# Doubling the self-attention keys over the partitions in the projection, from weights stored twice, in place of four SBUF transfers per head pair

## The chip, the cores and the metric

The kernel runs on one core of one Trainium2 chip. The metric is device time of one execution in microseconds (us). The core's engines are TensorE (PE in the profile, with its weight loads as PEld), VectorE (DVE), ScalarE (ACT), GpSimd (POOL) and SyncE (SP), which here only issues transfers to the 16 DMA engines.

## What is computed

Two decoder layers over x of shape 4 x 1024 x 256, one batch row after the other. The change touches one of the six blocks, the causal self-attention of the second layer, and the set-up of its weights:

```python
def _L1_attn_ref(x, w_q, w_k, w_v, w_o):          # w_*: 16 heads x 64 x 256
    q = jnp.einsum('bsd,hqd->bhsq', x, w_q)
    k = jnp.einsum('bsd,hqd->bhsq', x, w_k)
    v = jnp.einsum('bsd,hvd->bhsv', x, w_v)
    scores = jnp.einsum('bhsq,bhtq->bhst', q, k)
    ...
    weights = jax.nn.softmax(masked / jnp.sqrt(jnp.float32(dq)), axis=-1)
    out = jnp.einsum('bhst,bhtv->bhsv', weights, v)
    return jnp.einsum('bsf,df->bsd', cat, w_o)
```

The other blocks (an attention on random features, a cross-attention and a mixture of experts in layer 0, a cross-attention and a quantized gated network in layer 1) are the same before and after.

## The kernel before

**Precision.** Products of float32 numbers are built from two rounded parts, an upper and a lower one. `mm3` (L231) issues three matmuls per product: upper by upper, upper by lower, lower by upper. So a projection of 512 tokens with 256 inputs takes 2 x 3 = 6 matmuls of 128 x 512 (L233 to L235).

**The stage.** Heads are worked in eight pairs; a pair's projection fills 128 partitions, 64 for each head. The scores of a head must multiply (upper q + lower q) by k. The contraction of a matmul runs over the partitions, and a head has only 64 values, so a head's upper q lies on one half of the partitions and its lower q on the other (L1348, L1441). The keys must then be there twice, once on each half. The upper keys come by transfers: ScalarE copies the projection of the pair from PSUM into `l_x` (L1344; `l_x` is a part of `xn`, and the trace calls it xn), and SP issues four transfers per head pair (`l_dup`, L1508), which write each head's 64 rows to both halves of `l_k1`. The lower keys `l_k2` stand on their own half alone; the other half is zero, set by GpSimd at the stage's start.

**Steps and slots.** A head pair is one step of 16 blocks of 128 queries (two heads, eight blocks in the order 7, 0, 6, 1, 5, 2, 4, 3). I call the place k = 0 to 15 of a block in its pair a slot. A block passes: scores on PE (L1268 to L1270), row maximum on DVE (L1382), exponential on ACT (L1333), upper half-precision part on POOL (L1491), lower part on DVE (L1388), a DMA transpose (`l_flip`, L1500), and the product with the values on PE (L1286). Each engine runs its own list in order, written out by hand. In slot k PE issues the scores of the block six ahead, then a side task if the slot has one, then the product with the values of block k. DVE takes the maximum of the block six ahead, the side task's part, then the lower part of the block four ahead. SP issues the transpose of the block four ahead, then whatever else stands in that slot.

**Side tasks** (`l_tasks`, L1133) make what the next pair needs: K and Q (two each, one per 512 tokens), T (the output turned, two), and four of V (odd pairs) or O (even pairs from 2 on). All go through one PSUM bank, number 5. For each, PE waits until the task before has left the bank (L1305), issues its matmuls (`l_make`), ACT copies the upper part (`l_make_upper`), and DVE takes the lower part and frees the bank (`l_make_lower`). In pair 0 only K and Q have side tasks. The last pair has tasks of the next block in place of K and Q.

**Start.** Before the first scores the tasks of `FIRST_BANK` run: K, Q and V of the first pair, each in a bank of its own.

**Set-up.** The weights are split into parts once, and SP stores them to DRAM (`setup_split_sp`, L1769). ACT waits for these stores before `x_a_kv` in the first batch row (L1984). The stage loads a pair's weights from there, 512 KB at a time (`l_load_w`, L1511).

## Time and profile before

| | |
|---|---|
| Time, median of 3 runs | 3016.09 us (3014.46 to 3021.33) |
| Profiled execution, its own time | 3017.71 us |
| Its span, first to last instruction | 3016.0 us |
| Busy share of the span | PE 76%, DVE 72%, PEld 61%, ACT 35%, POOL 19% |
| Granted TensorE clock, mean | 0.864 of full speed |
| Head-pair steps 0 to 6 of the four stages | 279.3, 278.5, 282.7 and 278.1 us |

Times in the rows are microseconds from the span's start, unless marked ns. A step is counted from the first row maximum of one head pair to that of the next. The view of busy time by stretch has these columns: the stretch, its length, then busy time (and count of instructions) of PE, PEld, DVE, ACT and POOL, then the granted clock, the busy share of the DMA engines and the GB/s that they moved. In the groups by line, the number after the bar is the busy time, then the mean of one instruction in ns, then the engine's idle time just before these instructions and what ended it. On SP a row's time is that of issuing the transfer, not of the transfer.

### The profile page before, as it was taken

To read this page: it belongs to the slowest core of one execution; us is meant where nothing else is said; L and a number is where in the kernel's file an instruction comes from. 1 tells how busy PE (TensorE), PEld (TensorE's weight loads), DVE (VectorE), ACT (ScalarE), POOL (GpSimd) and SP (SyncE) were. 2 spreads that over 40 slices of the span, in tenths; PEclk is the share of its full clock that TensorE was granted. 3 is DMA by queue.
4 is the path that set the end of the run, shared out by engine and by line. 5 is a ranking of instruction groups with operands and counts; after the bars stand their busy time and mean duration, and the time that the engine had idled before them with its cause. 6 is when DMAs were issued, how large, how long until landed. Compare 5 with 4: busy or idle time off the path is not lost.

```text
span 3016.0 us, 50608 instructions
## 1 busy us (share of the span) xinstructions
PE 2279.5 (76%) x17454; PEld 1839.1 (61%) x17470; DVE 2179.1 (72%) x4246; ACT 1059.6 (35%) x2004; POOL 587.7 (19%) x666
## 2 busy tenths in 40 slices
PE   3668778868667778886777777887777777888875
PEld 3557666657455766665655666666556566666664
DVE  6765788867766578886776667888686756888766
ACT  2312444422522244442242234444134223444324
POOL 2011222212001122221201122222110102222120
PEclk8778899988778889998887789999887888999888
DMA  6001799830001089982000128997000014889600
GB/s 234 1 16 39 139 163 170 160 76 1 1 15 55 15 161 169 166 149 47 1 10 6 55 58 153 167 169 139 22 1 15 1 55 97 165 165 154 111 1 14
DMA packets 658403, 251.34 MB, mean 83 GB/s; under 512 B 613082, under 2 KB 633946, under 8 KB 657370
## 3 DMA queue, kind: packets, MB, share of 16 engines
q1 hardware_dynamic: 653978, 243.79, 41.2%
q10 hardware_dynamic: 4160, 4.19, 0.4%
q8 instruction: 144, 2.36, 0.3%
q14 instruction: 121, 0.99, 0.1%
...
## 4 chain that ended last, share of the span: by engine, by line
issue 32%; PE 26%; DVE 19%; DMA 11%; ACT 5%; POOL 4%; DVEq 1%; SPq 1%; ACTq 0%; POOLq 0%
PE ps L233 6%; DMA l_ptb<-l_phb 5%; PE ps L235 5%; PE ps L234 5%; DMA l_pts<-l_phs 4%; DVE nmax L1382 3%; POOL d_pn L990 2%; PE ps L1286 2%; DVE l_k L1437 1%; DVE l_phb L1388 1%; DVE l_q L1441 1%; PE ps L1268 1%; ACT l_q L1348 1%; DVE l_phs L1388 1%; DVE xn L284 1%
## 5 line engine op out<-in xcount | busy, mean ns | idle before, releaser
L1382 DVE TENSOR_REDUCE nmax<-ps 128x1 f32<-128x1024 f32 (+7 forms) x512 | 383.9, 751 | 25.9 <-PE ps L1270 23.8
L1491 POOL CAST l_phb<-l_pb 128x1024 f16<-128x1024 f32 (+3 forms) x256 | 240.1, 938 | 680.3 <-ACT l_pb L1333 356.1
L1333 ACT ACTIVATE l_pb<-ps,nmax 128x1024 f32<-128x1024 f32 (+3 forms) x256 | 244.5, 955 | 281.1 <-DVE nmax L1382 280.4
L1268 PE MATMUL ps<-l_k,l_q 128*128 128x512 f32 (+3 forms) x768 | 318.9, 415 | 26.4 <-ACT l_ps L1333 26.1
L1388 DVE TENSOR_TENSOR l_phb<-l_pb,l_phb 128x1024 f16<-128x1024 f32 (+3 forms) x256 | 287.5, 1123 | 22.4 <-POOL l_phb L1491 20.0
L1269 PE MATMUL ps<-l_k,l_q 128*128 128x512 f32 (+3 forms) x768 | 271.3, 364 | 0.0
L1286 PE MATMUL ps<-l_v,l_ptb 128*128 128x64 f16 x4992 | 199.1, 197 | 40.6 <-DMA l_ptb<-l_phb 40.2
L1286 PEld LDWEIGHTS ps<-l_v,l_ptb 128*128 128x128 f16 x4992 | 178.4, 101 | 73.9 <-DMA l_ptb<-l_phb 46.9
L233 PE MATMUL ps<-xTh,l_w 128*128 128x512 f32 x256 | 123.8, 483 | 85.2 <-DVE l_q L1441 50.4
L1268 PEld LDWEIGHTS ps<-l_k,l_q 128*128 128x128 f32 x768 | 156.5, 204 | 45.2 <-ACT l_ps L1333 31.7
L1491 POOL CAST l_phs<-l_ps 128x128 f16<-128x128 f32 (+3 forms) x256 | 127.1, 496 | 290.5 <-DMA l_pts<-l_phs 147.7
L1333 ACT ACTIVATE l_ps<-ps,nmax 128x128 f32<-128x128 f32 (+3 forms) x256 | 135.4, 529 | 111.4 <-DVE nmax L1382 110.3
L1269 PEld LDWEIGHTS ps<-l_k,l_q 128*128 128x128 f32 x768 | 157.5, 205 | 12.7
L985 POOL TENSOR_TENSOR x<-x,x_bo 128x2048 f32<-128x2048 f32 x8 | 36.2, 4519 | 562.7 <-DVE xn L284 562.7
L1388 DVE TENSOR_TENSOR l_phs<-l_ps,l_phs 128x128 f16<-128x128 f32 (+3 forms) x256 | 134.2, 524 | 14.3 <-POOL l_phs L1491 12.4
L316 ACT CAST xTh<-ps 128x512 fp32r<-128x512 f32 x80 | 45.4, 586 | 281.2 <-PE ps L303 281.2
L303 PE MATMUL ps<-idf,xn 128*128 128x128 f32 x320 | 66.0, 374 | 101.3 <-DVE xTl L322 61.4
L1437 DVE TENSOR_TENSOR l_k<-ps,xn 64x512 fp32r<-64x512 f32 x128 | 88.2, 689 | 74.8 <-ACT xn L1344 73.5
L1286 PE MATMUL ps<-l_v,l_pts 128*128 128x64 f16 x1920 | 105.7, 200 | 48.2 <-DMA l_pts<-l_phs 48.1
L1286 PEld LDWEIGHTS ps<-l_v,l_pts 128*128 128x128 f16 x1920 | 84.7, 102 | 89.5 <-DMA l_pts<-l_phs 53.0
L1441 DVE SCALAR_TENSOR_TENSOR l_q<-ps,l_q 64x512 fp32r<-64x512 f32 x128 | 88.2, 689 | 68.7 <-ACT l_q L1348 66.9
L1270 PE MATMUL ps<-causal,idb 128*128 128x128 bf16 x512 | 122.2, 239 | 0.0
...
## 6 DMA issues: line engine op xcount, KB each, us to landing
l_k<-xn SPq DMA_DIRECT2D x128, 256.0 KB, 4.1
...
xin<-in_x SPq DMA_DIRECT2D x4, 1024.0 KB, 5.4
...
m_w<-in_m_w SPq DMA_DIRECT2D x4, 1024.0 KB, 8.6
...
l_ptb<-l_phb SPq DMA_TRANSPOSE x256, 4.2
```

The costliest lines, as they stand in the source:

```text
L233: pe.matmul(o, lh, rh, start=start, stop=False)
L234: pe.matmul(o, lh, rl, start=False, stop=False)
L235: return pe.matmul(o, ll, rh, start=False, stop=stop)
L1268: pe.matmul(s[:, c0:c1], q, L["l_k1"][:, h, c0:c1], start=True, stop=False)
L1269: pe.matmul(s[:, c0:c1], q, L["l_k2"][:, j % 2, h, c0:c1], start=False, stop=c1 < n)
L1270: pe.matmul(s[:, n - P:n], idb[:], causal[:], start=False, stop=True).then_inc(q_["score"], 1)
L1286: last = pe.matmul(o, l_turned(k)[:, pp * (i + 1) + m, :], L["l_v"][:, (j // 2) % 2, vv, m, cols], start=m == 0 and n == 0, stop=m == i an ...
L1333: s.activation(l_numer(k)[:, 0:n], l_banks(k)[:, 0:n], ACT.Exp, bias=nmax[:, k % 4:k % 4 + 1], accum_out=lsum[:, h, k % NT:k % NT + 1]).th ...
L1382: v.tensor_reduce(nmax[:, k % 4:k % 4 + 1], l_banks(k)[:, 0:n], AX.X, ALU.max, negate=True).then_inc(q_["max"], 1)
L1388: v.tensor_tensor(l_parts(k)[:, n:2 * n], l_numer(k)[:, 0:n], l_parts(k)[:, 0:n], ALU.subtract).then_inc(q_["lo"], 1)
L1437: last = v.tensor_tensor(L["l_k2"][mine, n % 2, h, halves(g)], bank[mine, :], f32(l_x[mine, halves(g)]), ALU.subtract)
L1491: g.tensor_copy(l_parts(k)[:, 0:cols], l_numer(k)[:, 0:cols]).then_inc(q_["hi"], 1)
```

## The change

The weights of K are stored in DRAM with each head's 64 columns twice, so that a projection of one head fills all 128 partitions with two copies of its keys. K becomes four side tasks (head 0, tokens 0 to 511 and 512 to 1023, then head 1), each of six matmuls. ACT writes `l_k1` directly, DVE writes `l_k2` on all partitions, the four transfers and the zeroing go, a pair's load grows to 768 KB. The slots of the tasks change: Q to 0 and 1, K to 5, 7, 11 and 13, and O or V from 7, 9, 11, 13 to 9, 10, 12, 14. At the start K of head 1 comes last, after V.

```diff
@@ l_tasks
             if k in (0, 1):
-                return ("K", j + 1, k) if j + 1 < HP else None
+                return ("Q", j + 1, k) if j + 1 < HP else None
             if k in (2, 3):
                 return ("T", j - 1, k - 2) if j >= 1 else None
-            if k in (4, 5):
-                return ("Q", j + 1, k - 4) if j + 1 < HP else None
-            if k in (7, 9, 11, 13):
+            if k in (5, 7, 11, 13):
+                return ("K", j + 1, (5, 7, 11, 13).index(k)) if j + 1 < HP else None
+            if k in (9, 10, 12, 14):
                 if j % 2 == 0 and j >= 2:
-                    return "O", j // 2 - 1, (k - 7) // 2
+                    return "O", j // 2 - 1, (9, 10, 12, 14).index(k)
                 if j % 2 == 1 and j + 1 < HP:
-                    return "V", (j + 1) // 2, (k - 7) // 2
+                    return "V", (j + 1) // 2, (9, 10, 12, 14).index(k)
...
+        FIRST_BANK = {("Q", 0, 0): 4, ("Q", 0, 1): 7, ("K", 0, 0): 2, ("K", 0, 1): 3,
+                      ("V", 0, 0): 0, ("V", 0, 1): 1, ("V", 0, 2): 6, ("V", 0, 3): 5, ("K", 0, 2): 4, ("K", 0, 3): 7}
@@ l_make
+            elif kind == "K":
+                if (n, g) == (0, 2):
+                    pe.wait_ge(*lower(b, ("Q", 0, 1)))
+                for c in range(DC):
+                    w = 2 + 2 * (g // 2) + c
+                    last = mm3(pe, bank, L["l_w"][:, n % 2, 0, w, :], L["l_w"][:, n % 2, 1, w, :], xTh[:, c, halves(g % 2)], xTl[:, c, halves(g % 2)], c == 0, c == DC - 1)
@@ l_score
             if i == NT - 1:
-                pe.wait_ge(*lower(b, ("Q", j, 1)))
-                pe.wait_ge(q_[f"dup{h}"], (b * HP + j + 1) * 32)
+                pe.wait_ge(*lower(b, ("K", j, 2 * h + 1)))
@@ l_make_upper
-                if n >= 1 and g == 0:
-                    s.wait_ge(q_["dup0"], (b * HP + n) * 32)
-                    s.wait_ge(q_["dup1"], (b * HP + n) * 32)
-                last = s.copy(l_x[:, halves(g)], bank)
+                if n >= 1 and g % 2 == 0:
+                    s.wait_ge(q_["score"], b * NB + (n - 1) * NB1 + (g // 2 + 1) * NT)
+                last = s.copy(L["l_k1"][:, g // 2, halves(g % 2)], bank)
@@ l_make_lower
-                for h in range(2):
-                    mine, _ = own(h)
-                    last = v.tensor_tensor(L["l_k2"][mine, n % 2, h, halves(g)], bank[mine, :], f32(l_x[mine, halves(g)]), ALU.subtract)
+                last = v.tensor_tensor(L["l_k2"][:, n % 2, g // 2, halves(g % 2)], bank, f32(L["l_k1"][:, g // 2, halves(g % 2)]), ALU.subtract)
@@ l_sp
-                if j + 1 < HP and k == 4:
-                    l_dup(sp, b, j + 1, 0)
-                if j + 1 < HP and k == 10:
-                    l_dup(sp, b, j + 1, 1)
@@ setup_split_sp
+            def store_qk(part, made_of):
+
+                where = a["l_wqk_s"][:, part]
+                sp.dma_start(where[:, :, 0:DC * P], made_of[:, :, 0, :]).then_inc(s_ws, 16)
+                for h in range(2):
+                    for c in range(DC):
+                        for again in range(2):
+                            first = (2 + 2 * h + c) * P + again * SD
+                            sp.dma_start(where[:, :, first:first + SD], made_of[:, :, 1, c * P + h * SD:c * P + (h + 1) * SD]).then_inc(s_ws, 16)
```

The order of DVE's instructions around the tasks, in pair 1. Names: nmax is the row maximum, l_phb and l_phs the parts of large and small blocks, l_k the keys, l_q the queries, l_v the values. Before, slots 0 and 1:

```order
L1382 TENSOR_REDUCE nmax<-ps 128x1 [waits l_score]
L1423 REGISTER_ALU
L1437 TENSOR_TENSOR l_k<-ps,xn 64x512 [waits l_upper]
L1437 TENSOR_TENSOR l_k<-ps,xn 64x512
L1388 TENSOR_TENSOR l_phb<-l_pb,l_phb 128x768 [waits l_hi]
L1395 RECIPROCAL recs<-lsum 128x4 [waits l_exp]
L1396 REGISTER_ALU
L1400 TENSOR_TENSOR xn<-ps,recs 128x4x64 [waits l_pv,l_rc]
L1381 REGISTER_ALU
```

Of the change, slots 10 and 11 of the same pair (the line numbers have moved by a few):

```order
L1447 TENSOR_TENSOR l_v<-ps,l_v 128x512 [waits l_upper]
L1393 TENSOR_TENSOR l_phb<-l_pb,l_phb 128x640 [waits l_hi]
L1386 REGISTER_ALU
L1387 TENSOR_REDUCE nmax<-ps 128x1 [waits l_score]
L1428 REGISTER_ALU
L1440 TENSOR_TENSOR l_k<-ps,l_k 128x512 [waits l_upper]
L1393 TENSOR_TENSOR l_phs<-xn,l_phs 128x512 [waits l_hi]
```

A task of K that was two instructions on 64 partitions is one on 128, and tasks now stand in all six slots from 9 to 14 of an odd pair.

SP's order in pair 0, before, around slots 4 to 10 (DMA_TRANSPOSE is the transpose of a block):

```order
L1500 DMA_TRANSPOSE l_ptb<-l_phb 128x16x128 [waits l_pv,l_lo]
L1508 DMA l_k<-xn 64x1024 [waits l_score,l_upper]
L1508 DMA l_k<-xn 64x1024
L1500 DMA_TRANSPOSE l_pts<-l_phs 128x2x128 [waits l_pv,l_lo]
L1500 DMA_TRANSPOSE l_ptb<-l_phb 128x14x128 [waits l_pv,l_lo]
```

And of the change:

```order
L1497 DMA_TRANSPOSE l_ptb<-l_phb 128x16x128 [waits l_pv,l_lo]
L1497 DMA_TRANSPOSE l_pts<-l_phs 128x2x128 [waits l_pv,l_lo]
L1497 DMA_TRANSPOSE l_ptb<-l_phb 128x14x128 [waits l_pv,l_lo]
```

The two transfers that stood between the transposes, and the two in slot 10, are gone; nothing takes their place.

## Rows read from the trace of the kernel before

**Rows 1.** Busy time by stretch: seven steps together, then the first two alone

```profile
311.80:591.10 279.30, 222.29 (x2321) 177.12 (x2321) 229.51 (x354) 127.53 (x290) 75.97 (x110) 0.96 0.86 159
...
311.80:347.60 35.80, 26.89 (x226) 19.98 (x226) 28.61 (x43) 16.20 (x38) 11.10 (x15) 0.84 0.72 144
347.60:389.30 41.70, 32.20 (x336) 25.60 (x333) 32.63 (x51) 18.56 (x42) 10.44 (x16) 0.90 0.84 152
```

**Rows 2.** Groups by line, 311.8 to 591.1 (busy us, mean ns | idle before)

```profile
L1382 DVE TENSOR_REDUCE nmax<-ps 128x1 f32<-128x1024 f32 (+3 forms) x113 | 85.2, 755 | 5.0 <-PE ps L1270 4.5
L1388 DVE TENSOR_TENSOR l_phb<-l_pb,l_phb 128x1024 f16<-128x1024 f32 (+3 forms) x55 | 62.3, 1133 | 6.2 <-POOL l_phb L1491 5.6
L1388 DVE TENSOR_TENSOR l_phs<-l_ps,l_phs 128x128 f16<-128x128 f32 (+3 forms) x55 | 29.3, 533 | 3.4 <-POOL l_phs L1491 3.0
L233 PE MATMUL ps<-xTh,l_w 128*128 128x512 f32 x56 | 25.9, 463 | 20.7 <-DVE l_q L1441 12.6 <-DVE l_k L1437 5.4 <-ACT xin L1360 2.6
L1441 DVE SCALAR_TENSOR_TENSOR l_q<-ps,l_q 64x512 fp32r<-64x512 f32 x28 | 19.3, 689 | 15.3 <-ACT l_q L1348 14.9
L1437 DVE TENSOR_TENSOR l_k<-ps,xn 64x512 fp32r<-64x512 f32 x28 | 19.3, 689 | 13.9 <-ACT xn L1344 13.6
L1348 ACT ACTIVATE l_q<-ps 64x512 fp32r<-64x512 f32 x28 | 16.5, 591 | 23.5 <-PE ps L235 23.3
L1344 ACT CAST xn<-ps 128x512 fp32r<-128x512 f32 x14 | 8.2, 586 | 33.9 <-PE ps L235 33.9
```

**Rows 3.** Chain that ended last, 511 to 528 (start us, us, what)

```profile
511.00 5.39 DMA l_ptb<-l_phb
...
516.57 1.03 POOL l_phb L1491
...
517.71 4.66 DMA l_pts<-l_phs
...
523.73 0.28 PE ps L233
...
525.35 0.59 ACT xn L1344
525.97 0.06 DVE l_k L1437
...
527.41 0.50 PE ps L233
```

**Rows 4.** Timeline of DVE, 520 to 546 (in brackets: idle before, releaser)

```profile
525.97 1.39 DVE L1437 TENSOR_TENSOR l_k<-ps,xn 64x512 fp32r<-64x512 f32 x2 [1.38 <-ACT xn L1344]
...
537.98 1.39 DVE L1441 SCALAR_TENSOR_TENSOR l_q<-ps,l_q 64x512 fp32r<-64x512 f32 x2 [2.23 <-ACT l_q L1348]
```

**Rows 5.** Timeline of SP, 496 to 530

```profile
501.68 1.94 SPq L1500 DMA_TRANSPOSE l_ptb<-l_phb  x1
503.71 1.61 SPq L1508 DMA_DIRECT2D l_k<-xn  x2
505.41 1.96 SPq L1500 DMA_TRANSPOSE l_pts<-l_phs  x1
```

**Rows 6.** Timeline of DVE, 309 to 313: end of the stage's start

```profile
311.19 0.69 DVE L1444 TENSOR_TENSOR l_v<-ps,l_v 128x512 f16<-128x512 f32 x1 [0.73 <-ACT l_v L1358]
311.80 1.41 DVE L1382 TENSOR_REDUCE nmax<-ps 128x1 f32<-128x1024 f32 x2
```

**Rows 7.** Timeline of ACT, 30 to 125 (set-up)

```profile
86.07 0.35 ACT L831 COPY c_kT<-ps 128x256 f32<-128x256 f32 x1
...
96.62 0.63 ACT L602 ACTIVATE a_r<-a_r 32x512 f32<-32x512 f32 x1 [9.93 <-DVE a_r L676]
```

**Rows 8.** Timeline of SP, 0 to 200: last store of the set-up

```profile
53.92 1.24 SPq L1771 DMA_DIRECT2D l_wv_s<-s_lv  x1
```

**Rows 9.** DMA issues of the whole run: that store (KB, us to landing)

```profile
l_wv_s<-s_lv SPq DMA_DIRECT2D x1, 1024.0 KB, 8.8
```

**Rows 10.** DMA queues, 620 to 640, where only transposes run (packets, MB, share)

```profile
q1 hardware_dynamic: 9472, 2.36, 65.8%
```

More of the change, by code:

```diff
@@ L228, in decoder_kernel @@
         s_ws = sem("s_ws")
+        N_WS = 2 * (1 + 4 * DC) + 2
         def mm3(pe, o, lh, ll, rh, rl, start, stop):
@@ L1116, in decoder_kernel @@
             "w0", "w1", "wv", "wod",
-            "made", "upper", "lower", "dup0", "dup1",
+            "made", "upper", "lower",
             "score", "max", "exp", "rc",
             "hi", "lo", "pt0", "pt1", "pt2", "pt3", "pv",
-            "o", "wo", "zero")}
+            "o", "wo")}
         q_ = l_sem
@@ L1182, in l_numer @@
         def l_numer(k):
[L1183 removed]
+            return (L["l_pb"] if k % 2 == 0 else l_ps)[:, l_ring(k), :]
         def l_parts(k):
@@ L1204, in l_make @@
             bank = ps[:, l_bank(t), :]
-            if kind in "KQ":
-                if kind == "K" and g == 0:
+            if kind == "Q":
+                if g == 0:
                     pe.wait_ge(q_[f"w{n % 2}"], (b * NQ + n // 2 + 1) * 16)
-                m = "QK".index(kind)
                 for c in range(DC):
-                    last = mm3(pe, bank, L["l_w"][:, n % 2, 0, m, c, :], L["l_w"][:, n % 2, 1, m, c, :], xTh[:, c, halves(g)], xTl[:, c, halves(g)], c == 0, c == DC - 1)
+                    last = mm3(pe, bank, L["l_w"][:, n % 2, 0, c, :], L["l_w"][:, n % 2, 1, c, :], xTh[:, c, halves(g)], xTl[:, c, halves(g)], c == 0, c == DC - 1)
+            elif kind == "K":
[4 more added lines that the diff above has]
+                    last = mm3(pe, bank, L["l_w"][:, n % 2, 0, w, :], L["l_w"][:, n % 2, 1, w, :], xTh[:, c, halves(g % 2)], xTl[:, c, halves(g % 2)], c == 0, c == DC - 1)
             elif kind == "V":
@@ L1261, in l_score @@
             if g == 0:
-                pe.wait_ge(q_["zero"], b * 4 + 4)
                 pe.wait_ge(*lower(b, ("V", 0, 1)))
+            if g == 1:
+                pe.wait_ge(*lower(b, ("K", 0, 2)))
             s = l_banks(k)
@@ L1275, in l_pv @@
             if k == 0 and j % 2 == 0:
-                pe.wait_ge(*lower(b, ("V", j // 2, 3)))
+                pe.wait_ge(*lower(b, ("V", j // 2, 3) if j else ("K", 0, 3)))
             if k % 4 == 0 and g >= 8:
@@ L1476, in l_g @@
         def l_g(g, b):
-            g.wait_ge(s_xn, b * (NPH * NT) + 4 * NT)
-            for n in range(2):
-                for h in range(2):
-                    _, other = own(h)
-                    g.tensor_tensor(L["l_k2"][other, n, h, :], decay[other, :], decay[other, :], ALU.subtract).then_inc(q_["zero"], 1)
-                    g.wait_ge(q_["zero"], b * 4 + 2 * n + h + 1)
             for n in range(NB):
@@ L1500, in l_flip @@
             sp.dma_start_transpose(l_turned(k)[:, 0:2 * (i + 1), :], l_parts(k)[:, 0:2 * (i + 1) * P]).then_inc(q_[f"pt{g % 4}"], 16)
-        def l_dup(sp, b, j, h):
-            mine, _ = own(h)
-            sp.wait_ge(*upper(b, ("K", j, 1)))
-            if j >= 1:
-                sp.wait_ge(q_["score"], b * NB + (j - 1) * NB1 + (h + 1) * NT)
-            for o in (slice(0, 64), slice(64, 128)):
-                sp.dma_start(f32(L["l_k1"][o, h, :]), f32(l_x[mine, :])).then_inc(q_[f"dup{h}"], 16)
         def l_load_w(sp, b, j):
-            sp.dma_start(f32(L["l_w"][:, j % 2]).rearrange("p l m c e -> p l (m c e)"), a["l_wqk_s"][:, :, j, :]).then_inc(q_[f"w{j % 2}"], 16)
+            sp.dma_start(f32(L["l_w"][:, j % 2]).rearrange("p l m e -> p l (m e)"), a["l_wqk_s"][:, :, j, :]).then_inc(q_[f"w{j % 2}"], 16)
         def l_load_wv(sp, b, q):
@@ L1524, in l_sp @@
             l_load_wo(sp, b, 0)
-            for h in range(2):
-                l_dup(sp, b, 0, h)
             for g in range(4):
@@ L1532, in l_sp @@
                     l_flip(sp, b, g + 4)
-                if j + 1 < HP and k == 4:
-                    l_dup(sp, b, j + 1, 0)
-                if j + 1 < HP and k == 10:
-                    l_dup(sp, b, j + 1, 1)
                 if j + 2 < HP and k == 2:
-                    sp.wait_ge(*lower(b, ("Q", j + 1 - 1, 1)))
+                    sp.wait_ge(*lower(b, ("K", j, 3)))
                     l_load_w(sp, b, j + 2)
@@ L1983, in _ @@
                 if t == 6:
-                    s.wait_ge(s_ws, 64)
+                    s.wait_ge(s_ws, N_WS * 16)
                     x_a_kv(s, C0, 0)
```

21 lines of the change are left out of this document (9 added, 12 removed).

## The prediction

> **What bounds the kernel now.** I read the busy time by stretch first, to find out which engine is full where the change works. The stage's seven steps take 279.3 us, 39.9 each; DVE is busy for 229.5 of them, PE for 222.3, ACT for 127.5, and the DMA engines for 86% [rows 1]. No engine is full; DVE is nearest. So I read next what DVE waits for, in the groups by line. Of its 49.8 us idle, 15.3 stand before the lower parts of Q (L1441) and 13.9 before those of K (L1437), 29.2 together or 4.2 per step. The three groups of a block's own work have 14.6 before them (5.0, 6.2, 3.4), 2.1 per step [rows 2].
>
> The chain and the timeline say why. A task is a link through one bank: the six matmuls of a K task start at 523.73, ACT copies at 525.35, DVE begins at 525.97, that is 2.24 us from start to DVE, and PE can begin the next task only when DVE is through, at 527.41 [rows 3]. DVE, in order, stood idle 1.38 us for that one, and 2.23 us for the Q task that follows the two T tasks [rows 4]. Before this K task the chain is made of transposes: one of 5.39 us, a 1.03 us cast on GpSimd that needed its buffer, one of 4.66 us [rows 3]. So a step has two halves: slots 0 to 5, where six tasks stand in a row and the bank sets the pace, and slots 6 to 15, where transposes do. The four key transfers lie in the second. SP spends 1.61 us on a pair of them, and the transpose behind is issued at 505.41, when the one ahead was done at 503.62 [rows 5].
>
> **The change, part by part.** I count the change in DVE's idle time per step, since DVE's own work stays: four K instructions of 0.69 us per step before (28 in seven steps), four of the same length after, if 128 partitions cost what 64 do; the groups of the page of 128 x 512 on DVE are near it, as the values' 0.69 us [rows 2, 6].
>
> Slots 0 to 3 hold Q, Q, T, T after the change. The first Q takes the place of the K with 1.38 us. That wait came from the late transpose, of which I expect half gone; ACT's second instruction adds 0.59 us [rows 2]. I take 0.9 us for it. The second Q has a whole slot of DVE work ahead and I take 0.5. The Q that waited 2.23 us behind two T tasks is gone from there. K in slots 5 and 7 has free slots ahead: 0.15 each. Together 1.7 us in place of 4.2.
>
> Slots 9 to 14 become the crowded place. After a link of 2.24 us DVE adds 0.69, so two successive tasks of K or V are 2.93 us apart at least. DVE's own work per slot is a maximum of 0.755, a lower part (mean of 1.133 and 0.533) of 0.83, the task's 0.69 and a share of the finish that I estimate at 0.15: 2.43 [rows 2]. So each link costs about 0.5 us of idle time. Odd pairs (V) have five links, 2.5 us; even pairs from 2 on (O, which has no copy on ACT) have only the two into K, 1.0; pair 0 has K in 11 and 13 alone, 0.5.
>
> The transfers that go give back part of the 2.1 us before a block's own work. I take a third, 0.7, because T and the bank cause some of it, and because the larger K wait is counted already.
>
> Per step: V pairs -4.2+1.7+2.5-0.7 = -0.7; O pairs -4.2+1.7+1.0-0.7 = -2.2; pair 0 -4.2+1.7+0.5-0.7 = -2.7. A batch row has three, three and one of them: -11.4 us.
>
> The stage's start grows. Twelve more matmuls stand ahead of the first scores. In the chain the third to the sixth of a task are about 0.24 us apart (523.73 to 525.35 for six with the wait), so 2.8 us. Their two lower parts (1.4 us) fit behind them. Today DVE goes from the last V at 311.19 to the first maximum at 311.80 without a gap [rows 6], so I count +2.9 us, nothing hidden. A batch row gains 8.5 us, four rows 34.
>
> At nothing I put: PE's twelve more matmuls per step, 2.8 us (the granted clock is 0.96 of full here [rows 1]), in the 8.1 us per step in which PE is idle (57.0 of 279.3); without that cover they cost 2.8 x 28 = 78 us. ACT's two more copies, 1.2 us, in its 21.7 us idle per step. The zeroing on GpSimd, which ran ahead of the first maximum unseen. The larger weight load, since it is issued a whole pair ahead; its 256 KB more is a quarter of the 1 MB of keys that goes. The new waits of K on earlier scores: PE has issued those scores slots earlier.
>
> The set-up gets eighteen stores for two. The last store is issued at 53.92 and lands 8.8 us later, at 62.7 [rows 8, 9]. ACT comes to its wait at 86.07, and its next instruction waits for DVE until 96.62, 9.93 us; so stores may end at about 95.9 for nothing [rows 7]. The doubled keys are 16 x 1024 packets of 256 bytes. Transposes of the same stage move 9472 packets in 65.8% of 20 us on 16 engines, 22.2 ns each [rows 10]; at that price 16384 packets take 22.7 us, and the stores end at 85.4, even if nothing is taken off for what they replace. I count 0. For the Trainium skill, "DMA: Bandwidth & Descriptors", section "Specifications", a transfer under 512 bytes makes the engine read, modify and write. No row here has such small writes to DRAM. As a mechanism of this kernel, twice the price per packet would end the stores at 108.1, and ACT would stand 12.2 us, once. By the page the sum would be 12 us more.
>
> Sum: 3017.7 - 34 = 2983.7 for the profiled execution, which lies 1.6 above the median: 2982 us.
>
> **The rivals.** (1) Slower: the crowded bank. If PE is late in slots 9 to 14, because it must also issue the scores and the value products between two tasks (its busy time without tasks is about 1.2 us per slot: 31.8 per step less 24 projection matmuls at 0.24 and about 6 us for the other tasks), a link is up to 4.1 us, not 2.9. A batch row has 3x5 + 3x2 + 1 = 22 links. At +0.39 us per link (3.3 us) the 8.5 us are gone; from there on the change is slower. At +0.7 us it gives 3016 + 4 x (22 x 0.7 - 8.5) = 3044; at the full 1.2, 3088. For it speaks that PE would be 87% busy in a step; against it, that ACT and DVE need 1.3 us of a link in which PE may do just that work.
>
> (2) The transfers were the bound of the second half. Then all 2.1 us go, and the shorter queue also hides the links by half (22 x 0.25 = 5.5): 2982 - 4 x (7 x 1.4 + 5.5) = 2921. For it: the transposes in the chain, DMA at 86%. Against it: DVE is nearly without a gap in that half.
>
> (3) The transfers were hidden, and only the tasks' places count: relief 0 and the first Q waits its 1.38 + 0.59. 2982 + 4 x 7 x (0.7 + 1.1) = 3032 at worst, 3002 if only the relief fails.
>
> (4) The set-up stores cost twice the transposes' price per packet or more: 2994, and at four times the price, which ends them at 153.5, 3040. The rule of the skill's page named above is the reason to ask. For it speaks that no packet of this size goes to DRAM in this trace; against it, that 33 us lie free between 62.7 and 95.9.
>
> **How the numbers follow.** Measurements of this kernel tell about 0.2%, 6 us, from no change. Chances: my forecast 0.45 (2950 to 3005 as its own range), the crowded bank 0.25 (3010 to 3090), the bound transfers 0.12, hidden transfers 0.12 (about 3002 to 3032), the stores 0.06. Faster are my forecast but for a tenth of it, the bound transfers, and half of the last two: 0.60 in round numbers. Same 0.13, slower 0.27. The extreme bounds: all idle time before tasks and blocks gone except Q's 1.7 is -4.6 per step, 2899; links at their full price 3088. The range that leaves out 2 in 10 is 2930 to 3045.
>
> **What will show it.** Right: per step DVE idle before Q near 1.4 us and before K near 1.5, steps of even pairs shorter by 2 us, of odd pairs by less than 1; the start longer by 2.9; ACT's copy c_kT still at 86. Wrong: if the odd pairs' steps grow past 41 us with PE's first matmul of a task waiting for DVE in slots 9 to 14; if the transposes take the same 5 us from issue to landing without the key transfers; or if c_kT comes after 96.

## The result: slower, and the profile after

The changed kernel takes 3091.9 us in the median (3075.8 to 3103.2, 4 runs) against 3018.6 us for the kernel before on the same chip: a ratio of 1.023, with an interval of 1.020 to 1.026. I had forecast 2982 us and a range up to 3045, so the direction was wrong and the time lies outside my range. The profiled execution took 3098.5 us, and the rows of after are from it.

First the busy time by stretch, as in [rows 1]: seven steps, then the first three apart.

```profile
317.50:612.30 294.80, 242.93 (x2382) 193.44 (x2382) 222.23 (x350) 134.01 (x302) 84.94 (x110) 0.94 0.76 133
317.50:355.50 38.00, 27.22 (x228) 20.63 (x228) 26.94 (x41) 16.41 (x38) 10.87 (x16) 0.82 0.71 135
355.50:393.00 37.50, 31.50 (x338) 25.04 (x334) 30.24 (x50) 19.05 (x43) 11.37 (x16) 0.95 0.89 148
393.00:437.60 44.60, 36.59 (x370) 29.59 (x369) 33.34 (x54) 20.05 (x45) 12.87 (x18) 0.96 0.79 139
```

The seven steps take 294.8 us for 279.3. DVE, which was nearest to full, is busy 7 us less, and PE 21 us more. The second step is shorter than its 41.7 of before; the third to the sixth take 44.6 to 45.9, and the seventh, during which no weights are loaded, 39.5.

Then the groups by line over the same steps, which answer to [rows 2].

```profile
L1387 DVE TENSOR_REDUCE nmax<-ps 128x1 f32<-128x1024 f32 (+3 forms) x112 | 83.7, 749 | 7.1 <-PE ps L1276 6.9
L1393 DVE TENSOR_TENSOR l_phb<-l_pb,l_phb 128x1024 f16<-128x1024 f32 (+3 forms) x55 | 57.2, 1041 | 4.1 <-POOL l_phb L1488 3.8
L1393 DVE TENSOR_TENSOR l_phs<-xn,l_phs 128x128 f16<-128x128 f32 (+3 forms) x55 | 30.1, 547 | 13.1 <-POOL l_phs L1488 12.8
L1444 DVE SCALAR_TENSOR_TENSOR l_q<-ps,l_q 64x512 fp32r<-64x512 f32 x28 | 19.3, 689 | 14.7 <-ACT l_q L1353 14.5
L1440 DVE TENSOR_TENSOR l_k<-ps,l_k 128x512 fp32r<-128x512 f32 x27 | 18.6, 691 | 12.7 <-ACT l_k L1349 12.5
L1447 DVE TENSOR_TENSOR l_v<-ps,l_v 128x512 f16<-128x512 f32 x12 | 8.3, 691 | 14.0 <-ACT l_v L1363 14.0
```

DVE's idle time before Q and K is 27.4 us, 3.9 a step where my signs had 2.9 (1.4 for Q, 1.5 for K). Before a block's own work it grew from 14.6 to 24.3 us.

The gaps between row maxima in the trace give the length of each slot. This table is the mean over pairs 1 to 5 and the four batch rows, worked out in the same way for kernels that are introduced below:

| us | slots 0-6 | 7-8 | 9-14 | 15 | step |
|---|---|---|---|---|---|
| before | 22.6 | 3.8 | 12.7 | 1.5 | 40.6 |
| after | 17.1 | 7.2 | 19.1 | 1.0 | 44.3 |
| after, pair 6 (no weight load) | 16.9 | 4.3 | 17.0 | 0.9 | 39.2 |
| loads in slot 8 | 17.3 | 4.3 | 17.5 | 1.0 | 40.1 |
| before, no transfers | 21.6 | 3.7 | 12.0 | 0.8 | 38.1 |
| the same + 12 matmuls | 21.6 | 3.8 | 14.3 | 0.9 | 40.4 |
| before + 12 matmuls | 22.0 | 3.8 | 14.5 | 0.9 | 41.2 |
| before, own half on ScalarE | 21.8 | 3.8 | 12.0 | 0.8 | 38.4 |
| after, Q back in 4 and 5 | 20.6 | 3.9 | 15.8 | 1.0 | 41.4 |
| no transfers, new order | 18.4 | 5.8 | 14.0 | 0.8 | 39.0 |

The first half, slots 0 to 6, gives back 5.5 us, more than the 2.5 of the forecast. The loss is in two places, +3.4 us in slots 7 and 8 and +6.4 in slots 9 to 14. Over the 127 gaps of a batch row it adds up to 335.1 us for 319.3: four times 15.8 is 63 of the 81 us between the profiled executions. The rest lies between the stages. Pairs 1, 3 and 5, which have V tasks, and pairs 2 and 4, which have O tasks, now take the same 44 us a step; my sum had the V pairs 1.5 us longer.

**Slots 7 and 8.** SP's timeline shows a load of 768 KB and one of 256 KB issued just ahead of two transposes.

```profile
464.10 1.42 SPq L1497 DMA_TRANSPOSE l_ptb<-l_phb  x1
465.58 0.60 SPq L1500 DMA_DIRECT2D l_w<-l_wqk_s  x1
466.23 0.61 SPq L1506 DMA_DIRECT2D l_wo<-in_l_wo  x1
466.94 1.26 SPq L1497 DMA_TRANSPOSE l_pts<-l_phs  x1
468.30 4.39 SPq L1497 DMA_TRANSPOSE l_ptb<-l_phb  x1
```

PE's timeline shows what follows from it.

```profile
470.70 0.40 PE L236 MATMUL ps<-xTh,l_w 128*128 128x512 f32 x1
473.13 0.52 PE L1292 MATMUL ps<-l_v,l_pts 128*128 128x64 f16 x12 [2.03 <-DMA l_pts<-l_phs]
...
475.31 1.46 PE L1292 MATMUL ps<-l_v,l_ptb 128*128 128x64 f16 x24 [0.87 <-DMA l_ptb<-l_phb]
476.58 0.78 PE L1274 MATMUL ps<-l_k,l_q 128*128 128x512 f32 x1
...
478.46 0.41 PE L234 MATMUL ps<-l_wv,xTh 128*128 128x256 f32 x1
...
482.44 0.28 PE L234 MATMUL ps<-l_wv,xTh 128*128 128x256 f32 x1
```

PE waits 2.03 and 0.87 us for the two transposes, and then runs slowly: the same matmul of 256 columns takes 0.41 us at 478.46 and 0.28 at 482.44. The windows below give the granted clock of slots 7 and 8, 0.76 of full.

**Slots 9 to 14.** Windows of a V pair (first) and an O pair (second), before:

```profile
469.70:483.00 13.30, 9.39 (x118) 7.97 (x118) 11.25 (x18) 6.28 (x14) 3.52 (x5) 1.00 1.01 168
509.96:522.40 12.44, 10.50 (x114) 8.44 (x112) 11.04 (x18) 4.78 (x11) 3.85 (x5) 1.00 1.07 176
```

and after (slots 7 and 8 of the V pair, then slots 9 to 14 of both):

```profile
470.91:477.97 7.06, 4.16 (x46) 3.24 (x46) 4.15 (x9) 2.23 (x7) 1.68 (x3) 0.76 1.14 201
477.97:498.22 20.25, 18.81 (x175) 16.00 (x175) 13.04 (x21) 8.02 (x18) 4.96 (x7) 0.92 0.64 91
524.46:543.36 18.90, 18.38 (x155) 14.70 (x155) 13.41 (x20) 6.07 (x14) 5.41 (x7) 0.97 0.65 99
```

Before, DVE was busy 11.0 of the 12.4 us of the O pair and PE 10.5. After, PE is busy 18.4 of 18.9 us and DVE 13.4. Another engine has become full. That PE is busy does not yet say that its work sets the pace, since it may only do what fits between links; the experiments below decide that.

**The start and the set-up.** DVE's timeline at the end of the stage's start answers to [rows 6]: the two late K tasks are two more links of 1.4 us, and the first maximum comes at 317.53 for 311.80. But DVE's last instruction ahead of the stage (L323, L322 before) stands 3.5 us later too, at 299.49 for 295.98, so the start itself grew by 2.2 us. The other 3.5 us are no part of the change: kernels 1 and 2 below, which have the same program up to there, reach the first maximum at 320.22 and 314.75.

```profile
314.12 0.69 DVE L1447 TENSOR_TENSOR l_v<-ps,l_v 128x512 f16<-128x512 f32 x1 [0.72 <-ACT l_v L1363]
315.51 0.69 DVE L1440 TENSOR_TENSOR l_k<-ps,l_k 128x512 fp32r<-128x512 f32 x1 [0.70 <-ACT l_k L1349]
316.92 0.69 DVE L1440 TENSOR_TENSOR l_k<-ps,l_k 128x512 fp32r<-128x512 f32 x1 [0.71 <-ACT l_k L1349]
317.53 1.21 DVE L1387 TENSOR_REDUCE nmax<-ps 128x1 f32<-128x1024 f32 x1
```

The set-up's stores, on SP's timeline and in the list of transfers, answer to [rows 8, 9], and ACT's copy to [rows 7]:

```profile
42.72 10.52 SPq L1764 DMA_DIRECT2D l_wqk_s<-s_lqkh  x8
...
54.49 11.67 SPq L1764 DMA_DIRECT2D l_wqk_s<-s_lqk  x8
...
67.44 1.00 SPq L1754 DMA_DIRECT2D l_wv_s<-s_lv  x1
```

```profile
l_wqk_s<-s_lqkh SPq DMA_DIRECT2D x8, 256.0 KB, 4.6
l_wqk_s<-s_lqk SPq DMA_DIRECT2D x8, 256.0 KB, 5.2
l_wqk_s<-s_lqkh SPq DMA_DIRECT2D x1, 1024.0 KB, 4.6
```

```profile
85.86 0.35 ACT L832 COPY c_kT<-ps 128x256 f32<-128x256 f32 x1
```

The last store is issued at 67.4, some 14 us later than before, and ACT comes to its copy at 85.9 as it did. The stores delayed nothing there.

### The profile page after: what moved, and what is told of

Same layout as the page of the kernel before. It is cut to its first block, busy times and chain, and to the rows that moved or that the text cites. A ratio compares the mean times of both kernels' runs of the same rounds, so it can differ in the third digit from the quotient of the medians.

```text
span 3096.8 us, 51356 instructions
## 1 busy us (share of the span) xinstructions
PE 2368.9 (76%) x17854; PEld 1902.9 (61%) x17854; DVE 2164.9 (70%) x4246; ACT 1094.5 (35%) x2068; POOL 594.6 (19%) x650
## 4 chain that ended last, share of the span: by engine, by line
PE 34%; issue 29%; DVE 17%; DMA 7%; ACT 5%; POOL 4%; DVEq 1%; SPq 1%; ACTq 0%; POOLq 0%
PE ps L234 7%; PE ps L236 5%; PE ps L235 5%; DMA l_ptb<-l_phb 3%; PE ps L1253 3%; PE ps L1292 3%; DMA l_pts<-l_phs 2%; PE ps L1274 2%; DVE nmax L1387 2%; POOL d_pn L991 2%; PE ps L1275 2%; DVE l_q L1444 2%; DVE l_k L1440 1%; ACT l_q L1353 1%; ACT l_k L1349 1%
## 5 line engine op out<-in xcount | busy, mean ns | idle before, releaser
L1488 POOL CAST l_phb<-l_pb 128x1024 f16<-128x1024 f32 (+3 forms) x256 | 268.9, 1050 | 941.1 <-ACT l_pb L1339 617.9
L1387 DVE TENSOR_REDUCE nmax<-ps 128x1 f32<-128x1024 f32 (+7 forms) x512 | 382.7, 749 | 21.8 <-PE ps L1276 20.7
L1274 PE MATMUL ps<-l_k,l_q 128*128 128x512 f32 (+3 forms) x768 | 315.8, 411 | 32.9 <-ACT xn L1339 32.5
L1393 DVE TENSOR_TENSOR l_phb<-l_pb,l_phb 128x1024 f16<-128x1024 f32 (+3 forms) x256 | 269.8, 1054 | 18.6 <-POOL l_phb L1488 17.0
L1275 PE MATMUL ps<-l_k,l_q 128*128 128x512 f32 (+3 forms) x768 | 267.5, 360 | 0.0
L234 PE MATMUL ps<-xTh,l_w 128*128 128x512 f32 x384 | 173.7, 452 | 52.7 <-DVE l_q L1444 35.8
L1488 POOL CAST l_phs<-xn 128x128 f16<-128x128 f32 (+3 forms) x256 | 132.9, 519 | 334.9 <-ACT xn L1339 194.9
L1274 PEld LDWEIGHTS ps<-l_k,l_q 128*128 128x128 f32 x768 | 153.5, 200 | 51.2 <-ACT xn L1339 39.2
L1339 ACT ACTIVATE xn<-ps,nmax 128x128 f32<-128x128 f32 (+3 forms) x256 | 135.7, 530 | 111.5 <-DVE nmax L1387 109.3
L1393 DVE TENSOR_TENSOR l_phs<-xn,l_phs 128x128 f16<-128x128 f32 (+3 forms) x256 | 139.7, 546 | 48.9 <-POOL l_phs L1488 48.1
L235 PE MATMUL ps<-xTl,l_w 128*128 128x512 f32 x384 | 156.4, 407 | 0.0
L236 PE MATMUL ps<-xTh,l_w 128*128 128x512 f32 x384 | 155.7, 405 | 0.0
```

The lines of the kernel that those rows point to most:

```text
L234: pe.matmul(o, lh, rh, start=start, stop=False)
L235: pe.matmul(o, lh, rl, start=False, stop=False)
L236: return pe.matmul(o, ll, rh, start=False, stop=stop)
L1274: pe.matmul(s[:, c0:c1], q, L["l_k1"][:, h, c0:c1], start=True, stop=False)
L1275: pe.matmul(s[:, c0:c1], q, L["l_k2"][:, j % 2, h, c0:c1], start=False, stop=c1 < n)
L1339: s.activation(l_numer(k)[:, 0:n], l_banks(k)[:, 0:n], ACT.Exp, bias=nmax[:, k % 4:k % 4 + 1], accum_out=lsum[:, h, k % NT:k % NT + 1]).th ...
```

## The experiments

Each run was timed beside the kernel before, whose median in the four groups of runs was 3020.5, 3022.5, 3024.9 and 3020.8 us. I compare through the ratios; 0.1% is 3 us, and the intervals are about 0.2% to either side.

**Theories.** A: the loads. They stand in slot 2 as ever, but the row of tasks in slots 0 to 5, which gave PE work while transposes waited behind a load, has lost its two Q tasks. B: my rival, the crowded bank: the length of a link sets slots 9 to 14. C: PE's own work sets them.

**1. Loads later.** In the changed kernel (this is called kernel 1 from here on, and so with the others):

```
-                if j + 2 < HP and k == 2:
+                if j + 2 < HP and k == 8:      (the three loads alike)
```

> The changed kernel with its steady weight loads issued in slot 8 of a head pair in place of slot 2. Theory A (the load delays the transposes of slots 6 to 8, since no Q task covers it any more): slots 7 and 8 of pairs 1 to 5 fall by about 3.6 us together, so 24 steps x 3.6 us less than the changed kernel's 3092 us, 2990 to 3020 us. Theory B (only the crowded bank 5 in slots 9 to 14 costs): no change against the changed kernel, 3080 to 3100 us, and slots 7 and 8 stay long. If the load does the same harm wherever it stands, the time also stays, with the loss in slots 10 to 13.

It took 3006.1 us, ratio 0.9954 [0.9936, 0.9972]: 2.8 points less than the changed kernel's 1.023, or 83 us. Slots 7 and 8 fell from 7.2 to 4.3 us, 2.9 of the 3.6 that I expected, and slots 9 to 14 fell by 1.6, which I had not expected; the last section says what part of the gain is waiting and what part is clock. In pairs 1 to 5 the loss does not come back in the slots behind slot 8. There the tasks keep PE at work while transposes wait: a transpose behind this load lands 6.4 us after its issue, and PE does not wait for it. In pair 0, which has no V or O tasks, slots 9 to 14 do grow, from 11.7 to 14.2 us. A holds. And the changed kernel with this one edit is faster than before by 0.5%.

**2. No loads at all.** The three loads are taken out, with their waits set to the first load of a batch row.

> The changed kernel without any weight load inside the stage (pairs 2 to 7 work with the weights of pairs 0 and 1, the output differs). It is the whole price of the loads: theory A says 3.6 us a step and 24 steps, 3000 us or a little under; theory B says under 10 us of gain, 3080 us or more. Set beside the kernel with late loads it says whether late loads are free.

2984.7 us, ratio 0.9889 [0.9868, 0.9909]. The loads cost 3.4 points, 103 us, in the changed kernel; in slot 8 they still cost 20 us. Most of that is in pairs 0 and 1 (3.6 and 1.6 us of a batch row's 6.2). No run takes the loads out of the kernel before; there the pair without a load, pair 6, takes 40.0 us where the others take 40.6.

**3. Tasks spread.**

```
-            if k in (5, 7, 11, 13):     K
+            if k in (5, 6, 12, 13):
-            if k in (9, 10, 12, 14):    O or V
+            if k in (8, 9, 10, 14):
```

> The changed kernel with its tasks spread: K in slots 5, 6, 12, 13 and V or O in 8, 9, 10, 14 (before 5, 7, 11, 13 and 9, 10, 12, 14), the loads still in slot 2. Slots 7, 11 and 15 are free of tasks, so no run of the bank is longer than three. Theory B (the link of 3.1 us through bank 5 sets slots 9 to 14): slots 8 to 14 lose 2 to 4 us of some 21, 3000 to 3040 us in all. Theory A alone: no more than 15 us less, 3077 us or more.

3067.5 us, ratio 1.0163 [1.0139, 1.0186], 20 us less than the changed kernel. That is neither theory's number. Slots 9 to 14 fell from 19.1 to 15.8 us, but slots 0 to 6 rose by 1.9: part of what left the run of tasks came back ahead of it. Slots 7 and 8 stayed long, 6.8 us, though slots 6 and 8 have tasks here.

**4. Transfers out of the kernel before.** They stay for the first pair of each batch row alone; the waits for them are set to that pair.

```
-                if j + 1 < HP and k == 4:
-                    l_dup(sp, b, j + 1, 0)
-                if j + 1 < HP and k == 10:
-                    l_dup(sp, b, j + 1, 1)
```

> The kernel before without its key transfers after the first pair of each batch row (scores of pairs 1 to 7 use the first pair's upper keys, the output differs); its two K tasks stay. This is the relief by itself. My prediction took 0.7 us a step, 28 steps: 2997 us against 3017. The rival that the transfers were the bound says 2957 us or less. If they are hidden: 3010 us or more.

2937.8 us, ratio 0.9727 [0.9706, 0.9749]: the transfers cost 82 us, 2.9 us a step and not 0.7. PE's groups over the whole run say where. Of the kernel before:

```profile
L1286 PE MATMUL ps<-l_v,l_ptb 128*128 128x64 f16 x4992 | 199.1, 197 | 40.6 <-DMA l_ptb<-l_phb 40.2
L1286 PE MATMUL ps<-l_v,l_pts 128*128 128x64 f16 x1920 | 105.7, 200 | 48.2 <-DMA l_pts<-l_phs 48.1
```

and without the transfers:

```profile
L1286 PE MATMUL ps<-l_v,l_ptb 128*128 128x64 f16 x4992 | 195.7, 196 | 35.8 <-DMA l_ptb<-l_phb 35.3
L1286 PE MATMUL ps<-l_v,l_pts 128*128 128x64 f16 x1920 | 103.0, 197 | 1.8 <-DMA l_pts<-l_phs 1.7
```

The wait for the small blocks' transposes, 48.2 us, all but vanishes. The median time from issue to landing does not show this: it goes from 4.2 to 4.1 us for the transposes of large blocks and from 3.4 to 3.0 for those of small ones. A few late ones made the wait.

**5 to 7. What sets slots 9 to 14.** Three edits of kernel 1 (loads in slot 8). In 5 the K tasks of slots 7 and 13 are gone from pair 2 on. In 6 the ACT and DVE parts of the K tasks of slots 11 and 13 take 64 columns from pair 2 on, PE's work stays. In 7 those K tasks make one product of three. The edit of kernel 7:

```
+                    if n >= 1 and g >= 2:
+                        last = pe.matmul(bank, L["l_w"][:, n % 2, 0, w, :], xTh[:, c, halves(g % 2)], start=c == 0, stop=c == DC - 1)
+                        continue
```

That of kernel 6, on ACT (DVE's is alike):

```
+                wide = slice(g % 2 * HALF, g % 2 * HALF + (HALF if n < 2 or g < 2 else 64))
-                last = s.copy(L["l_k1"][:, g // 2, halves(g % 2)], bank)
+                last = s.copy(L["l_k1"][:, g // 2, wide], bank[:, 0:wide.stop - wide.start])
```

> The kernel with the late loads (3006 us), in which two of the four K tasks (those of slots 7 and 13) are left out from pair 2 on, 24 steps in all; the scores use stale keys in those halves, the output differs. It is the price of the two added tasks. The kernel without loads takes 39.7 us a step and the kernel before without transfers 37.9, so by that 1.8 us x 24 = 43 us less, 2955 to 2970 us. If the added tasks are covered by waiting that is there anyway (my zero for their matmuls, and a crowded bank that costs little): 2990 us or more.

> The kernel with the late loads, in which ScalarE and VectorE take 64 of 512 columns in the K tasks of slots 11 and 13 from pair 2 on (stale keys beyond, the output differs); TensorE's work is the same. If the length of the link through bank 5 sets slots 9 to 14 (my crowded bank), two links a step are some 0.8 us shorter, 24 x 1.6 = 38 us less, 2960 to 2975 us. If TensorE's own work sets them, nothing or up to 10 us: 2995 to 3006 us.

> The kernel with the late loads, in which the K tasks of slots 11 and 13 make 2 of their 6 matmuls (upper part by upper part alone; keys of the second head less exact). Both links and TensorE's work get shorter by 8 matmuls of some 0.22 us a step, 28 steps. Both theories say 40 to 50 us less if every matmul is on the path, 2955 to 2965 us; less than 20 us says that neither sets slots 9 to 14 alone. Read beside the narrow parts: if those give nothing and this gives 40 us, TensorE's work is the price.

Kernel 5: 2949.4 us, ratio 0.9765 [0.9738, 0.9792], 57 us less than kernel 1, 2.4 us for each of 24 steps. Kernel 6: 2978.7 us, 0.9864 [0.9835, 0.9893], 27 us less, between B's 38 and C's 10. Kernel 7: 2983.4 us, 0.9876 [0.9849, 0.9902], 24 us less, half of what its 8 matmuls a step would be if all were on the path. So both theories hold in part. The windows of slots 9 to 14 of kernel 1, a V pair and an O pair, show why:

```profile
470.15:487.80 17.65, 15.99 (x164) 13.23 (x162) 12.90 (x21) 8.12 (x18) 4.50 (x6) 1.00 1.01 163
509.64:526.55 16.91, 16.39 (x149) 13.09 (x148) 13.07 (x22) 6.07 (x14) 5.54 (x7) 1.00 0.97 199
```

PE is busy 16.4 of 16.9 us in the O pair, and waits before O for DVE's part of K, 0.25 and 0.27 us. In the V pair it waits for DVE before every task behind the first:

```profile
471.57 0.39 PE L234 MATMUL ps<-l_wv,xTh 128*128 128x256 f32 x1 [0.23 <-DVE l_v L1447]
474.65 0.50 PE L234 MATMUL ps<-xTh,l_w 128*128 128x512 f32 x1 [0.45 <-DVE l_v L1447]
477.71 0.38 PE L234 MATMUL ps<-l_wv,xTh 128*128 128x256 f32 x1 [0.25 <-DVE l_k L1440]
480.79 0.50 PE L234 MATMUL ps<-xTh,l_w 128*128 128x512 f32 x1 [0.47 <-DVE l_v L1447]
483.86 0.38 PE L234 MATMUL ps<-l_wv,xTh 128*128 128x256 f32 x1 [0.27 <-DVE l_k L1440]
```

These tasks start 3.06 to 3.08 us apart, which is the link's length. So the link sets the V pair with little idle time left on PE, and in the O pair PE is nearly full. A shorter link removes such waits, less work removes the rest, and after either the other is left.

**8. One task earlier.** Kernel 1 with O or V in slots 8, 10, 12, 14.

> The kernel with the late loads, with V and O in slots 8, 10, 12, 14 in place of 9, 10, 12, 14. One task leaves the run of six; VectorE is busy 20.8 of 21.6 us in slots 0 to 8 and takes 0.7 us more there, TensorE is full in slots 9 to 14 and gets some 1.5 us less there. If TensorE sets slots 9 to 14: 0.8 us a step, 2980 to 2990 us. If the number of links in a row sets them: the same direction, 2.9 us less there and 0.7 to 2 more in slot 8, 2955 to 2985 us. No change (3000 to 3010) says that the price is the same wherever the task stands.

3013.0 us, ratio 0.9964 [0.9945, 0.9984]: no change against kernel 1. Slots 9 to 14 gave up 1.4 us and slots 7 and 8 took 1.5. The task has the same price in slot 8 as in slot 9.

**9. Small loads.** The changed kernel, loads in slot 2, with 4 of 6 weight blocks (512 KB) from pair 2 on.

> The changed kernel, loads in slot 2 as it stands, but from pair 2 on each weight load brings 512 KB, as before, and not 768 KB (the second head's keys use stale weights, the output differs). It tells the size of the load from the loss of its cover. If the size is what costs (the step of my prediction that put the larger load at nothing): slots 7 and 8 fall back to 4 us, 3010 to 3025 us. If the cover is what was lost (the Q tasks no longer stand in slots 4 and 5): a third of the 86 us that the late loads gave, 3055 to 3075 us.

3068.2 us, ratio 1.0156 [1.0132, 1.0180]: 22 us less, in the middle of what the lost cover predicted. The size is a fifth of the loads' price of 103 us, and a quarter of what moving them gives; with the intervals it can be ten us more or less.

**10. Half of the transfers.** The kernel before, in which ACT copies the half that stays on its partitions and only the other goes by DMA:

```
-            for o in (slice(0, 64), slice(64, 128)):
-                sp.dma_start(f32(L["l_k1"][o, h, :]), f32(l_x[mine, :])).then_inc(q_[f"dup{h}"], 16)
+            sp.dma_start(f32(L["l_k1"][other, h, :]), f32(l_x[mine, :])).then_inc(q_[f"dup{h}"], 16)
...
+            s.copy(L["l_k1"][mine, h, :], l_x[mine, :]).then_inc(q_["own"], 1)      (ACT, slots 6 and 10)
```

> The kernel before with two key transfers a pair in place of four: the half of each head's keys that stays on its partitions is copied by ScalarE (64 x 1024, in slots 6 and 10), only the other half goes by DMA. Leaving all four out gave 83 us. If bytes on the queue are the price: half of it, 40 us less, 2970 to 2985 us. If ScalarE's two copies of some 1.1 us delay exponentials: 0.5 to 1 us a step back, 2990 to 3010 us. If the number of transfers ahead of a transpose is all and their bytes nothing: also half.

2953.7 us, ratio 0.9776 [0.9754, 0.9797]. It beats both kernels, by 68 and 138 us, and does better than any of my numbers: leaving out half of the transfers gives 82% of what leaving out all four gives. What ACT's 64 copies cost, if anything, is within the 15 us between this kernel and kernel 4. PE's wait for the small blocks' transposes went from 48.2 to 12.0 us. In its groups:

```profile
L1370 ACT CAST l_k<-xn 64x1024 fp32r<-64x1024 f32 x64 | 66.5, 1039 | 0.8
L1287 PE MATMUL ps<-l_v,l_pts 128*128 128x64 f16 x1920 | 103.5, 198 | 12.0 <-DMA l_pts<-l_phs 11.9
```

**11 and 12. My zero for the twelve matmuls.** The kernel before, with its transfers (11) and without them (12), with two groups of six matmuls on bank 5 in slots 10 and 12, whose result nothing reads:

```
+                if g // NB1 + 1 < HP and g % NB1 in (10, 12):
+                    j = g // NB1
+                    pe.wait_ge(*lower(b, past))                 (the task made last)
+                    for c in range(DC):
+                        mm3(pe, ps[:, 5, :], L["l_w"][:, (j + 1) % 2, 0, 1, c, :], L["l_w"][:, (j + 1) % 2, 1, 1, c, :], xTh[:, c, 0:HALF], xTl[:, c, 0:HALF], c == 0, c == DC - 1)
```

> The kernel before, with its transfers, and with 12 extra matmuls of 512 columns a step on bank 5 in the free slots 10 and 12 (their result is read by no one). It prices my zero for PE's twelve matmuls where I took it from: if TensorE's idle time in slots 9 to 14, which the late transposes cause, covers them, 3015 to 3030 us. If they are on the path: 12 x 0.233 = 2.8 us a step, 28 steps, up to 3098 us.

> The kernel before without its transfers after the first pair (2938 us, output differs) and with the same 12 extra matmuls a step. If the matmuls are hidden only while transfers make TensorE wait, they cost here what the two added K tasks cost (57 us over 24 steps, so up to 66 over 28): 2990 to 3010 us. If they are hidden here too: 2938 to 2950 us.

Kernel 11: 3033.6 us, ratio 1.0038 [1.0020, 1.0056], 11 us more than before. Kernel 12: 2993.6 us, ratio 0.9900 [0.9878, 0.9921], 52 us more than kernel 4. The same matmuls cost four to five times as much where the transfers are gone. PE's busy time in slots 9 to 14 shows it. Kernel 11, kernel 4 and kernel 12, a V pair each:

```profile
471.56:485.80 14.24, 13.97 (x151) 11.71 (x152) 10.99 (x19) 6.37 (x15) 4.50 (x7) 1.00 1.03 178
```

```profile
462.72:474.99 12.27, 10.61 (x135) 9.22 (x135) 11.26 (x18) 6.31 (x15) 3.91 (x6) 1.00 0.86 141
```

```profile
465.23:479.45 14.22, 13.63 (x148) 11.30 (x148) 11.38 (x18) 6.31 (x14) 4.33 (x6) 1.00 0.79 127
```

Before, this stretch took 13.30 us with PE busy for 9.39. The added matmuls went into that idle time, and the stretch grew by 0.9. Without transfers it grew by 1.95. The mean over pairs 1 to 5 is less clear-cut, 1.8 and 2.3 us; in kernel 11 slots 0 to 6 and slot 15 give back another 0.6 us each. With the matmuls in place the stretch is nearly as long with the transfers as without them, 14.5 and 14.3 us: once PE is full there, the transposes' delay costs little, and taking it away gains little. Over the whole kernel the transfers still cost 42 us with the matmuls in place (kernel 11 less kernel 12), where they cost 82 without them; 25 of the 42 are in pair 0, 42.3 and 36.0 us, which has no V or O tasks.

**13 and 14. The order of the tasks.** The changed kernel with Q in slots 4 and 5, K in 1, 6, 12, 14 and V or O in 8, 9, 11, 13 (13); and kernel 4 with the new order (Q 0, 1; K 5, 7; V or O 9, 10, 12, 14) and nothing doubled (14). Loads stay in slot 2.

> The changed kernel, loads in slot 2, with its tasks nearer to the order of before: Q back in slots 4 and 5, K in 1, 6, 12, 14, V or O in 8, 9, 11, 13. If the Q tasks in slots 4 and 5 are what covered the loads, slots 7 and 8 of pairs 1 to 5 fall from 7.3 us to some 4 us, and slots 0 to 6 go back up from 17 to some 21 us, since the cover is time that TensorE spends anyway: near the sum of the kernel before without transfers (2938) and the price of the doubled tasks (57 to 66), 2995 to 3030 us. If the loads cost the same under any order: slots 7 and 8 stay at 7 us, 3090 us or more.

> The kernel before without its transfers after the first pair (2938 us, output differs), with the order of the changed kernel: Q in slots 0 and 1, K in 5 and 7, V or O in 9, 10, 12, 14; loads of 512 KB in slot 2; nothing is doubled. The kernel with small loads (3068 us) less the doubled tasks (57 to 66) says 3000 to 3015 us: so the order alone would cost 60 to 75 us, all of it in slots 7 to 9 behind the loads. If the order costs nothing without doubled tasks: 2930 to 2950 us.

Kernel 13: 3017.9 us, ratio 0.9997 [0.9977, 1.0017]. The order brings back 70 us. Slots 7 and 8 are 3.9 us where they were 7.2, behind loads in the same slot 2, and slots 0 to 6 are 20.6. K and V have moved too, and slots 9 to 14 went from 19.1 to 15.8 us. But kernel 3 also had K in slot 6 and V or O in slot 8, with Q left in 0 and 1, and its slots 7 and 8 stayed at 6.8 us. So the move of Q back to slots 4 and 5 is what covers the loads. Whether it does so by the work itself or by the time that it gives the load (slots 0 to 6 take 20.6 us here, 19.0 in kernel 3) is not separated. Kernel 14: 2962.9 us, ratio 0.9805 [0.9777, 0.9834]: the order alone costs 24 us, where I had expected 60 to 75. Slots 7 and 8 lose 2.1 us and slots 9 to 14 lose 2.0 against kernel 4, and slots 0 to 6 gain 3.2.

## Why the prediction was wrong

By rows of this table each next kernel differs in one main part; the step to kernel 9 also has the longer start and the stores:

| kernel | ratio | step by step |
|---|---|---|
| before | 1.000 | |
| transfers out (4) | 0.973 | -82 us |
| new order of tasks (14) | 0.981 | +24 |
| keys doubled, four K tasks for two, loads still 512 KB (9) | 1.016 | +106 |
| loads of 768 KB (the change) | 1.023 | +22 |

**"PE's twelve more matmuls: nothing"** is the first step that failed, and the larger. I put them into the 8.1 us per step in which PE is idle, without asking where in the step that time lies. By slots, from the same traces (mean over pairs 1 to 5, us a step; the clock is the granted one, as a share of full):

| | PE idle, slots 0-6 | 7-8 | 9-14 | 15 | PE busy | clock |
|---|---|---|---|---|---|---|
| before | 4.3 | 0.0 | 2.4 | 0.2 | 33.7 | 0.96 |
| before, no transfers | 4.5 | 0.0 | 1.0 | 0.0 | 32.7 | 0.98 |
| before + 12 matmuls | 4.2 | 0.1 | 0.6 | 0.0 | 36.3 | 0.97 |
| no transfers + 12 matmuls | 4.2 | 0.1 | 0.3 | 0.0 | 35.9 | 0.98 |
| after | 3.3 | 2.9 | 1.2 | 0.0 | 36.9 | 0.96 |
| loads in slot 8 | 3.2 | 0.2 | 1.2 | 0.0 | 35.4 | 1.00 |

Of 7.0 us idle before, 4.3 lie in slots 0 to 6, and most of that before the first matmul of a task that waits for the bank (20.7 us in seven steps [rows 2]). Two of the four K tasks, and one V or O task more than before, came to slots 9 to 14, and there only 2.4 us are idle. The change itself takes these away: without transfers 1.0 is left. Kernels 11 and 12 show the same matmuls at 11 and at 52 us. I had named the price without cover, 78 us, but did not ask whether the change itself removes the cover. In slots 9 to 14 the relief from the transfers and the cover for the matmuls are the same idle time, and only one of them can be had.

**"The larger weight load: nothing, since it is issued a whole pair ahead"** is the second. I had looked at when the load is needed, not at what is queued behind it. The loads cost 103 us in the changed kernel. A quarter of what moving them gives is their size (22 us, kernel 9); the rest is that Q left slots 4 and 5, where it had kept PE and DVE at work while the transposes stood behind the load (kernels 13 and 3).

**"The transfers give back 0.7 us per step"** was mis-sized: 2.9 us (kernel 4). I had read DVE's idle time before a block's own work, 2.1 us. What the transfers delay is seen from PE, which waits for the transposes. In pairs 1 to 5 a step gets 2.5 us shorter: PE is idle for 1.5 less, and its same matmuls take 1.0 less, at a granted clock of 0.98 for 0.96. I had no term for the clock. My rival of bound transfers was right about this part, with 2921 us for a kernel that got the relief and kept it.

**Links.** The link is as I worked it out: the start of a V task is 2.9 to 3.1 us ahead of the next. But DVE's idle time is 3.9 us a step before K and Q, and V's 14.0 us are 4.7 for each of three V pairs, where I had 0.5 for each of V's links. In the V pair of kernel 1, DVE is busy 12.90 us in six slots, 2.15 a slot and not 2.43, and a link takes 3.07 us and not 2.93; that makes 0.9 us idle for a link. For the O pairs I had counted two links and no work of PE, and PE turned out nearly full there. The rival of the crowded bank gave 3044 to 3088 us, near the result, with PE's scores and products between two tasks as its reason, and links of up to 4.1 us, which are not seen. Kernel 6 says that the links' length is worth 27 us of the loss; kernel 12, that PE's added work by itself is worth 52 where nothing covers it. So the rival had the right place and part of the cause, and its number came near by luck; it did not have the loads.

**The stage's start**, +2.9 us a batch row: 2.2 us in the first row, so about right. The gaps from a batch row's last row maximum to the next one's first grew by 1, 8 and 2 us. The 8 is more than a start can hold; what the rest of it is I have not separated.

**The set-up stores**, 0 us: right. My estimate of their price was 22.7 us for all at the transposes' price per packet; they took 22.2 us of SP's time, in sixteen transfers. But small pieces do cost here. Below are 4 us of the kernel before, in which a store of 2 MB goes to DRAM in pieces of 16 KB, and 3 us of the changed one, in which only pieces of 256 bytes go:

```profile
44.00:48.00 4.00, 4.00 (x18) 3.26 (x18) 1.82 (x4) 2.00 (x1) 4.00 (x1) 0.71 1.02 430
46.50:49.50 3.00, 2.50 (x9) 1.95 (x8) 3.00 (x1) 0.00 (x0) 3.00 (x1) 0.50 0.87 217
```

The DMA engines move 217 GB/s in place of 430, busy for 0.87 of the time in place of all of it. By the Trainium skill, "DMA: Bandwidth & Descriptors", section "Specifications", a transfer under 512 bytes is a read, a modify and a write; the rows agree with it in direction, and no run here separates it from the price of a piece. That section gives no price; the doubling in my prediction was my own. The last store lands at some 76 us, 10 us ahead of ACT's copy.

**The first half**, slots 0 to 6: 5.5 us a step gained in the forecast's place. It was not a gain by itself: kernel 13 gives 3.5 of them back and is 70 us faster, since that time had covered the loads.

**The signs.** DVE's idle time per step is 2.1 us before Q and 1.8 before K, for 1.4 and 1.5. Of the signs of being wrong, two came true: steps of odd pairs grew past 41 us, though those of even pairs did as well, and the transposes' median from issue to landing hardly moved, 4.1 and 3.1 us for 4.2 and 3.4. The second was a poor sign, since the same medians go with the 82 us of kernel 4.

The 106 us of the table and the 57 of kernel 5 look apart, since both are two K tasks. The slots bring them nearer. Kernel 5 left out a task of slot 7, which gave 0.4 us, and one of slot 13, and slots 9 to 14 fell by 1.8. Between kernels 14 and 9 both added tasks stand in slots 9 to 14, which go from 14.0 to 18.3 us; with the loads out of the way (kernel 1) they are 17.5, so 1.8 for each of the two tasks.

What stays open: the other 0.8 us of these slots; some 15 us of the 106 that lie between the stages; and why leaving out half of the transfers gives more than half of the relief.
